# Spacing the indirect scatters of two routed layers with a small GpSimd clear

## The chip, the cores and the metric

The kernel runs on one core of one Trainium2 chip. The metric is the device time of one execution in microseconds (us). The engines are named as in the profile: PE is TensorE, PEld its weight loads, ACT is ScalarE, DVE is VectorE, POOL is GpSimd, SP is SyncE, which here only issues DMAs.

## What is computed

A two-layer transformer stack over 4096 tokens (16 sequences of 256) of width 128, all in float32. Each layer is an attention-like part and a feed-forward part that routes every token to a few experts, and each part is normalised and added to the residual:

```
x = x + layernorm(L0_attn(layernorm(x)))        # sorted-kernel attention, 16 heads
x = x + layernorm(L0_ffn(layernorm(x)))         # routed: 32 experts, top 4, gated SiLU, hidden 128, plus a shared one
x = x + layernorm(L1_attn(layernorm(x)))        # RWKV time mix and channel mix
x = x + layernorm(L1_ffn(layernorm(x)))         # routed: 8 experts, top 2, SiLU, hidden 512, plus a shared one
return x
```

The routed part of layer 0, cut:

```
logits = flat @ router_w.T + router_bias
topk_scores, topk_idx = top_k(softmax(logits), 4);  topk_scores /= topk_scores.sum()
h = silu(flat @ gate_w[e].T) * (flat @ up_w[e].T)
out = sum over the 4 chosen e of score * (h @ down_w[e].T)
out = out + silu(flat @ sgate_w.T) * (flat @ sup_w.T) @ sdown_w.T
```

## The kernel before

`build` runs the stages one after another, and `routed` builds both routed layers, with `layer` 0 (called gated) or 1. Only `routed` is touched.

The tokens stand in SBUF as 32 tiles of 128 tokens (`TILES`), in 8 groups of 4 (`GROUPS`, `TPG`), and are routed in two parts of 16 tiles each (`PT`). For each part DVE picks the experts (`choose`), counts them (`bases`) and works out the row of a sorted buffer to which each token goes (`place`). The end of `place` raises the semaphore `placed` (L1391). POOL waits for it (L965) and then scatters: for each tile and each chosen expert it issues one indirect DMA (L968) that writes the 128 rows of 512 bytes of a tile of `h_tok` to their places in the DRAM buffer `xs[part]`. That makes 16 tiles times 4 choices, 64 transfers, for a part of layer 0, and 32 for a part of layer 1. A run of such transfers is called a burst below.

In the meantime PE, ACT and DVE work on the shared expert: `shared_first` (L1031, three matmuls for each product, L1027 to L1029), ACT's SiLU (`shared`, L1220 in layer 0, L1224 in layer 1), in layer 0 DVE's product (L1416), and `shared_second` (L1052). There are 32 such units in a layer (`SU`). The three engines hand the work to each other by semaphores that each matmul group, activation and product raises: `gate_ps` and `up_ps` by PE for ACT and DVE, `sum_ps` by PE for DVE and ACT, `hidden_ready` for PE. The routing steps of part 1 are mixed in: the transposes and router products of the second half of the tokens (`turn` L994, `route` L1006, ACT's `turned` L1208 and L1209), then `bases(1)`, `place(1)` and `table(1)` at fixed unit numbers (`AT_TOTALS`, `AT_RANKS`, `AT_OWNERS`). In layer 1 eight units (`EARLY`) come ahead of this second half.

After the last shared unit comes the routed stage. SP loads 512 rows at a time of `xs` (L924), first when all scatters of that part have landed (L921), four buffers ahead (`XB`). PE turns them (L1095) and ACT copies them out (L1252, `e_x_turned`): this is the start of one quad of the routed stage. There are 24 quads for a part in layer 0 and 10 in layer 1 (`JQ`). The results are stored to `ys` (L930). When those of part 0 are stored, POOL gathers them with indirect DMAs (L979) and adds tiles to the residual (`residual_add`, L215). The order on POOL is thus: scatters of part 0, scatters of part 1, gathers. The gathers of part 1 of layer 0 are made in the next stage, `rwkv` (L1910).

Of the kernel before, what the change touches and what calls it, by code (L numbers as in the profile page):

```python
# [15 lines left out]
P = 128  # L16
# [24 lines left out]
FROM = 1  # L41
# [49 lines left out]
def build(nc, a, out):  # L91
    top = ExitStack()
    with top:
# [157 lines left out]
        attention0(nc, a, locals())  # L251
        clear_semaphores(100)
        routed(nc, a, locals(), 0)
        clear_semaphores(90)
        rwkv(nc, a, locals())
        clear_semaphores(100)
        routed(nc, a, locals(), 1)


# [523 lines left out]
def routed(nc, a, env, layer):  # L783
# [4 lines left out]
    E, K, SH, WE = ((E0, K0, SH0, WE0), (E1, K1, CH1, WE1))[layer]  # L788
# [19 lines left out]
    with ExitStack() as s:  # L808
        def tb(name, cols, dt=F32, rows=P):
            return s.enter_context(nc.sbuf_tensor(pre + name, [rows, cols], dt))  # L810
# [4 lines left out]
        sem = lambda n: env["semaphore"](pre + n)  # L815
# [5 lines left out]
        w_down = tb("w_down", SH * P)  # L821
        w_all = tb("w_all", E * WE)
        router, bias = tb("router", E), tb("bias", E) if gated else None
        zeros = tb("zeros", P)
        scale_y, shift_y, shift_x = tb("scale_y", TILES), tb("shift_y", TILES), tb("shift_x", TILES)
        logits, left = tb("logits", PT * LW), tb("left", PT * LW)
        best, chosen, total = tb("best", PT * 8), tb("chosen", PT * 8), tb("total", PT)
# [58 lines left out]
        x_ps, x_sb, first_ps, t_silu, t_hidden, h_ps, h_sb, y_ps, y_sb = map(  # L886
            sem, ("x_ps", "x_sb", "first_ps", "t_silu", "t_hidden", "h_ps", "h_sb", "y_ps", "y_sb"))
        weighed, combined, own = sem("weighed"), sem("combined"), sem("own")
        normed, x_ready = sem("normed"), sem("x_ready")
        x_stats_done = sem("x_stats_done") if gated else sem("out_stored")  # L890

        def tile(x, t):
            return x[:, t * P:(t + 1) * P]
# [4 lines left out]
        with nc.Block() as block:  # L898
# [44 lines left out]
            @block.gpsimd  # L943
            def _(pool):
                nc.gpsimd.memset(zeros[:, :], 0.0).then_inc(zeros_made, 1)
                nc.gpsimd.memset(ones_bf[:, :], 1.0).then_inc(constants, 1)
                nc.gpsimd.memset(later[:, :], -1.0).then_inc(constants, 1)
                nc.gpsimd.memset(one_row[:, :], 1.0).then_inc(constants, 1)
                flow3 = flow[:, :].rearrange("p (e t) -> p e t", t=PT)
                nc.gpsimd.memset(flow3[:, :, 0:1], 0.0).then_inc(constants, 1)  # L950
                nc.gpsimd.memset(flow3[:, :, 1:PT], 1.0).then_inc(constants, 1)
                nc.gpsimd.iota(tile_start[:, 0:1], pattern=[[P * P, 1]], base=0, channel_multiplier=P,
                               allow_small_or_imprecise_dtypes=True).then_inc(constants, 1)
                pool.wait_ge(constants, FROM + 6)
                nc.gpsimd.affine_select(out=later[:, :], in_=later[:, :], compare_op=ALU.is_ge, fill=0.0, base=0,
                                        pattern=[[-1, P]], channel_multiplier=1).then_inc(constants, 1)
                for i, (n, c) in enumerate(SPLIT):
                    pool.wait_ge(staged, FROM + 16 * len(SPLIT))
                    nc.gpsimd.tensor_copy(w_hi[n][:, :], w_stage[i][:, :]).then_inc(hi_made, 1)
                    pool.wait_ge(hi_made, FROM + i + 1)  # L960
                    nc.gpsimd.tensor_tensor(w_lo[n][:, :], w_stage[i][:, :], w_hi[n][:, :].bitcast(F32),
                                            ALU.subtract).then_inc(lo_made, 1)
                pool.wait_ge(cleared, FROM + 16 * NP)
                for part in range(NP):
                    pool.wait_ge(placed, FROM + part + 1)  # L965
                    for t in range(part * PT, (part + 1) * PT):
                        for k in range(K):
                            nc.gpsimd.indirect_dma_start(  # L968
                                out=xs[part], out_offset=bass.IndirectOffsetOnAxis(ap=rows_of[:, t * K + k:t * K + k + 1], axis=0),
                                in_=tile(h_tok, t), in_offset=None, bounds_check=ROWS - 1).then_inc(scattered[t // TPG], 16)  # L970
                for part in range(OVER):
                    last = (part + 1) * JQ
                    for i in range(YB):
                        pool.wait_ge(stored[i], FROM + 16 * ((last - 1 - i) // YB + 1))
                    for t in range(part * PT, (part + 1) * PT):
                        if t >= GB:
                            pool.wait_ge(combined, FROM + t - GB + 1)
                        for k in range(K):
                            nc.gpsimd.indirect_dma_start(  # L979
                                out=got[t % GB][:, k * P:(k + 1) * P], out_offset=None, in_=ys[part],  # L980
                                in_offset=bass.IndirectOffsetOnAxis(ap=rows_of[:, t * K + k:t * K + k + 1], axis=0),
                                bounds_check=ROWS - 1).then_inc(gathered[t % GB], 16)
                        g = t // TPG
                        if t % TPG == TPG - 1 and g % GPP:
                            env["residual_add"](pool, g - 1, normed, x_ready)
                    env["residual_add"](pool, (part + 1) * GPP - 1, normed, x_ready)
# [1039 lines left out]
```

## Time and profile before

| | |
|---|---|
| time, median of 3 runs | 1696.18 us (1694.03 to 1700.94) |
| time of the profiled execution | 1706.38 us |
| its span, first to last instruction | 1704.6 us |
| mean granted clock of PE | 0.756 |
| busy: PE, DVE, ACT, POOL | 987.1, 844.1, 612.4, 496.3 us (58, 50, 36, 29%) |
| scatters of layer 0 (L968), 128 | 126.6 us busy on POOL |
| scatters of layer 1 (L968), 64 | 63.6 us busy on POOL |

No engine is busy for much more than half of the span. The page shows shares of the whole; the question for this change is what PE, ACT and DVE do while POOL scatters, and what they wait for then. An indirect DMA's row on POOL is the time in which POOL writes its descriptors, not the time of the transfer.

### The profile page before, as it was taken

How to read it: one execution, taken by the hardware profiler on the slowest of the kernel's cores; microseconds unless marked ns; L12 is line 12 of the kernel's file. 1: busy time of each engine (PE TensorE's matmuls, PEld its weight loads, DVE VectorE, ACT ScalarE, POOL GpSimd, SP SyncE). 2: the span in 40 equal slices, each digit the busy share in tenths (PEclk: the TensorE clock that was granted, in tenths of full speed). 3: DMA queues.
4: the chain of work that ended last, by engine and by line, in shares of the span. 5: the costliest groups of instructions: out<-in, count | busy, mean ns of one | idle time of the engine just before them, and what ended most of it. 6: DMA issues, size and time to landing. Idle time of an engine off the chain costs nothing. (4 is left out here: it accounts for less than half of the span.)

```text
span 1704.6 us, 20367 instructions
## 1 busy us (share of the span) xinstructions
PE 987.1 (58%) x5710; PEld 749.2 (44%) x5712; DVE 844.1 (50%) x2487; ACT 612.4 (36%) x1263; POOL 496.3 (29%) x598
## 2 busy tenths in 40 slices
PE   2865666642215822898667224666525484998840
PEld 1624555532214721777556113343315472776630
DVE  4497688874503500632356338998844220002525
ACT  2331566645202200333222226566434332553420
POOL 0001333321571275001562564000001534004435
PEclk9995665665557955999899657787766596998975
DMA  2000000009511011344343210000052201122221
GB/s 59 0 1 0 0 0 0 0 1 288 207 52 39 13 51 35 93 121 132 100 123 84 71 42 25 1 1 1 1 146 98 65 21 53 51 64 61 56 65 53
DMA packets 130722, 96.98 MB, mean 57 GB/s; under 512 B 11600, under 2 KB 121552, under 8 KB 129616
## 3 DMA queue, kind: packets, MB, share of 16 engines
q1 hardware_dynamic: 118352, 70.79, 14.3%
q0 software_dynamic: 12288, 25.19, 5.0%
q8 instruction: 41, 0.67, 0.2%
q14 instruction: 41, 0.34, 0.1%
HBM read 45.61 MB, written 50.33 MB: 56 GB/s over the span
## 5 line engine op out<-in xcount | busy, mean ns | idle before, releaser
L968 POOL DMA_INDIRECT e_xs<-h_tok,rows_of x128 | 126.6, 989 | 147.3 <-DVEq L1391 108.9
L1520 DVE COPY e_y_rows<-e_ps_y 128x512 f32<-128x512 f32 x68 | 47.0, 691 | 242.4 <-PE e_ps_y L1152 167.5
L1052 PE MATMUL e_ps_y<-e_w_down,e_hidden 128*128 128x128 f32 x512 | 77.3, 300 | 120.5 <-DVE e_hidden L1416 110.5
L1052 PEld LDWEIGHTS e_ps_y<-e_w_down,e_hidden 128*128 128x128 f32 x512 | 74.3, 213 | 130.8 <-DVE e_hidden L1416 65.8
L979 POOL DMA_INDIRECT e_got<-e_ys,rows_of x64 | 65.0, 1015 | 175.1 <-DMA e_ys<-e_y_rows 132.1
L979 POOL DMA_INDIRECT e_got<-e_ys,e_rows_of x64 | 66.0, 1031 | 151.1 <-DMA e_ys<-e_y_rows 132.7
L632 ACT ACTIVATE mask<-ps_q,k_neg 128x256 bf16<-128x256 f32 x256 | 100.4, 485 | 21.0 <-PE ps_q L725 21.0
L1104 PE MATMUL e_ps_gu<-e_w_all,e_x_turned 128*128 x384 | 103.3, 416 | 2.6 <-ACT e_x_turned L1252 1.7
L1416 DVE TENSOR_TENSOR e_hidden<-e_ps_gu,e_silu 128x512 f32<-128x512 f32 x32 | 22.0, 690 | 155.8 <-remote 118.8
L968 POOL DMA_INDIRECT e_xs<-h_tok,e_rows_of x64 | 63.6, 994 | 105.3 <-DVEq L1391 86.4
L725 PE MATMUL ps_q<-q_parts,pick 128*128 (+1 forms) x256 | 66.1, 400 | 44.7 <-DVE mask L553 41.5
L1152 PE MATMUL e_ps_y<-e_w_all,e_h_turned 128*128 x640 | 87.2, 281 | 7.8 <-issue 5.2
L1134 PE MATMUL e_ps_up<-e_w_all,e_x_turned 128*128 x160 | 85.7, 620 | 9.5 <-ACT e_x_turned L1252 9.5
L553 DVE TENSOR_TENSOR mask<-ps_q,k_tok 128x1024 bf16<-128x1024 f32 x64 | 75.3, 1218 | 27.6 <-PE ps_q L725 25.4
L1123 PE MATMUL e_ps_y<-e_w_all,e_h_turned 128*128 x384 | 60.1, 304 | 46.5 <-ACT e_h_turned L1268 28.2
L1258 ACT ACTIVATE e_silu<-e_ps_gu 128x512 f32<-128x512 f32 x48 | 28.7, 597 | 161.6 <-PE e_ps_gu L1104 119.1
L1910 POOL DMA_INDIRECT c_got<-e_ys,rows_of x64 | 66.6, 1040 | 61.5 <-POOLq L106 21.6
L1220 ACT ACTIVATE e_silu<-e_ps_gu 128x512 f32<-128x512 f32 x32 | 19.1, 597 | 181.8 <-remote 131.8
L1268 ACT ACTIVATE e_h_turned<-e_ps_h 128x512 f32<-128x512 f32 x128 | 75.9, 593 | 22.2 <-remote 11.3
L1152 PEld LDWEIGHTS e_ps_y<-e_w_all,e_h_turned 128*128 128x128 f32 x640 | 79.9, 196 | 8.9 <-issue 8.8
L1263 ACT ACTIVATE e_hidden<-e_ps_up 128x512 f32<-128x512 f32 x80 | 47.7, 597 | 99.3 <-PE e_ps_up L1134 85.3
L1104 PEld LDWEIGHTS e_ps_gu<-e_w_all,e_x_turned 128*128 128x128 f32 x384 | 74.6, 205 | 17.0 <-issue 5.0
(367 smaller groups left out, 2455.2 us busy)
## 6 DMA issues: line engine op xcount, KB each, us to landing
e_x_rows<-e_xs SPq DMA_DIRECT2D x68, 256.0 KB, 3.1
e_ys<-e_y_rows SPq DMA_DIRECT2D x68, 256.0 KB, 2.4
e_xs<-e_zeros SPq DMA_DIRECT2D x2, 6144.0 KB, 34.7
e_w_all<-in_w SPq DMA_DIRECT2D x4, 1536.0 KB
e_xs<-e_zeros SPq DMA_DIRECT2D x2, 2560.0 KB
e_w_all<-in_w SPq DMA_DIRECT2D x4, 1024.0 KB, 11.1
e_xs<-h_tok,rows_of POOLq DMA_INDIRECT x128
result<-x_tok SPq DMA_DIRECT2D x8, 256.0 KB
```

Of the source, the lines that this page charges most:

```text
L553: last = nc.vector.tensor_tensor(mask[parity][quad][j][:, :].rearrange("p (h t) -> p h t", t=T), psq[0][:, :].rearrange("p (h t) -> p h t" ...
L632: last = nc.scalar.activation(mask[u][QS // 2 + j][keys][:, h * T:(h + 1) * T], psq[1][:, h * T:(h + 1) * T], ACT.Sign, bias=k_neg[u][:, k ...
L725: last = nc.tensor.matmul(psq[0 if on_dve else 1][:, h * T:(h + 1) * T], pick[:, (quad * HQ + h) * P:(quad * HQ + h + 1) * P], q_parts[:, ...
L968: nc.gpsimd.indirect_dma_start(out=xs[part], out_offset=bass.IndirectOffsetOnAxis(ap=rows_of[:, t * K + k:t * K + k + 1], axis=0), in_=til ...
L979: nc.gpsimd.indirect_dma_start(out=got[t % GB][:, k * P:(k + 1) * P], out_offset=None, in_=ys[part], in_offset=bass.IndirectOffsetOnAxis(a ...
L1052: last = nc.tensor.matmul(ps_sum[g % len(ps_sum)][:, t * P:(t + 1) * P], hidden[n % 2][:, t * P:(t + 1) * P], w_down[:, i * P:(i + 1) * P] ...
L1104: last = nc.tensor.matmul(ps_gu[n % 2][:, t * 2 * P:(t + 1) * 2 * P], x_turned[n % 2][:, t * P:(t + 1) * P], at(w_all, col, 2 * P), start= ...
L1123: last = nc.tensor.matmul(ps_y[:, o], h_turned[n % 2][:, o], at(w_all, col + 2 * P, P), start=True, stop=True)
L1134: nc.tensor.matmul(ps_up[n % 2][:, :], x_turned[q % 2][:, t * P:(t + 1) * P], at(w_all, col, CH1 * P), start=True, stop=True).then_inc(fir ...
L1152: last = nc.tensor.matmul(ps_yy[q % 2][:, t * P:(t + 1) * P], h_turned[n % 2][:, i * P:(i + 1) * P], at(w_all, col + (CH1 + i) * P, P), st ...
L1268: nc.scalar.activation(h_turned[n % 2][:, :], (ps_h if gated else ps_hh[n % 2])[:, :], ACT.Copy).then_inc(h_sb, 1)
L1910: nc.gpsimd.indirect_dma_start(out=got[t % GB][:, k * P:(k + 1) * P], out_offset=None, in_=env["ys0"], in_offset=bass.IndirectOffsetOnAxis ...
```

## The change

One tile of 256 columns (`spacer`) and one semaphore (`spaced`) are added. In the scatter loop, after each indirect DMA is issued, POOL clears this tile with a memset and waits for the end of that memset before it goes on. The loop runs 128 times in layer 0 and 64 times in layer 1, so 192 memsets and 192 waits are added. The gathers are as they were.

```diff
-        zeros = tb("zeros", P)
+        zeros, spacer = tb("zeros", P), tb("spacer", 256)
...
-        normed, x_ready = sem("normed"), sem("x_ready")
+        normed, x_ready, spaced = sem("normed"), sem("x_ready"), sem("spaced")
...
                             nc.gpsimd.indirect_dma_start(
                                 out=xs[part], out_offset=bass.IndirectOffsetOnAxis(ap=rows_of[:, t * K + k:t * K + k + 1], axis=0),
                                 in_=tile(h_tok, t), in_offset=None, bounds_check=ROWS - 1).then_inc(scattered[t // TPG], 16)
+                            nc.gpsimd.memset(spacer[:, :], 0.0).then_inc(spaced, 1)
+                            pool.wait_ge(spaced, FROM + t * K + k + 1)
```

## Rows read from the trace of the kernel before

**Rows 1.** Groups of POOL's instructions by line and shape, whole span.
```profile
line engine op names shapes xcount | busy us, mean ns | idle before us <-releasers
L968 POOL DMA_INDIRECT e_xs<-h_tok,rows_of x128 | 126.6, 989 | 147.3 <-DVEq L1391 108.9 <-issue 38.4
L968 POOL DMA_INDIRECT e_xs<-h_tok,e_rows_of x64 | 63.6, 994 | 105.3 <-DVEq L1391 86.4 <-issue 18.9
...
L653 POOL MEMSET qn<- 64x256 f32 x1 | 0.3, 306 | 109.4 <-POOLq L315 109.4
```

**Rows 2.** Timeline of POOL: start, duration, instruction, idle time before it and releaser.
```profile
521.26 0.98 POOL L968 DMA_INDIRECT e_xs<-h_tok,rows_of  x1 [0.30 <-issue]
585.34 0.98 POOL L968 DMA_INDIRECT e_xs<-h_tok,rows_of  x1 [63.10 <-DVEq L1391]
...
666.38 0.98 POOL L968 DMA_INDIRECT e_xs<-h_tok,rows_of  x1 [0.31 <-issue]
...
1312.18 1.09 POOL L968 DMA_INDIRECT e_xs<-h_tok,e_rows_of  x1 [51.14 <-DVEq L1391]
...
1352.73 1.11 POOL L968 DMA_INDIRECT e_xs<-h_tok,e_rows_of  x1 [0.30 <-issue]
1389.12 0.98 POOL L968 DMA_INDIRECT e_xs<-h_tok,e_rows_of  x1 [35.28 <-DVEq L1391]
```

**Rows 3.** Busy time of each engine in stretches with and without scatters.
```profile
core 0: us, PE busy (x) PEld busy (x) DVE busy (x) ACT busy (x) POOL busy (x), PEclk, DMA share, GB/s
440.00:450.00 10.00, 0.00 (x0) 0.00 (x0) 9.31 (x40) 0.47 (x2) 7.56 (x9) 0.50 0.68 280
...
533.00:560.00 27.00, 26.93 (x155) 23.48 (x155) 16.98 (x76) 9.77 (x14) 0.00 (x0) 0.94 0.00 1
...
645.00:655.00 10.00, 0.00 (x0) 0.00 (x0) 0.00 (x0) 0.00 (x0) 7.56 (x9) 0.50 0.13 46
```

**Rows 4.** Timelines of PE, ACT and DVE about the scatters of layer 0.
```profile
479.51 0.63 PE L1029 MATMUL e_ps_gu<-e_h_hi,e_sgate_hi 128*128 128x512 f32 x1
...
475.64 0.60 ACT L1208 ACTIVATE e_h_hi<-e_ps_x 128x512 fp32r<-128x512 f32 x1 [12.99 <-remote]
...
527.47 0.60 ACT L1220 ACTIVATE e_silu<-e_ps_gu 128x512 f32<-128x512 f32 x1 [49.44 <-remote]
...
671.90 0.69 DVE L1416 TENSOR_TENSOR e_hidden<-e_ps_gu,e_silu 128x512 f32<-128x512 f32 x1 [36.41 <-remote]
...
685.85 0.60 ACT L1252 ACTIVATE e_x_turned<-e_ps_x 128x512 f32<-128x512 f32 x1 [3.67 <-PE e_ps_x L1095]
```

**Rows 5.** Timeline of ACT about the scatters of layer 1.
```profile
1351.17 0.60 ACT L1208 ACTIVATE e_h_hi<-e_ps_x 128x512 fp32r<-128x512 f32 x1 [15.63 <-DMA e_xs<-h_tok,rows_of]
...
1357.67 0.60 ACT L1224 ACTIVATE e_hidden<-e_ps_up 128x512 f32<-128x512 f32 x1 [4.11 <-remote]
...
1430.30 0.60 ACT L1252 ACTIVATE e_x_turned<-e_ps_x 128x512 f32<-128x512 f32 x1 [28.40 <-remote]
```

**Rows 6.** Timeline of ACT later in the routed stage of layer 0.
```profile
798.31 0.60 ACT L1252 ACTIVATE e_x_turned<-e_ps_x 128x512 f32<-128x512 f32 x1
```

**Rows 7.** Timelines of POOL and ACT at the ends of two gather bursts.
```profile
819.20 1.01 POOL L979 DMA_INDIRECT e_got<-e_ys,rows_of  x1 [0.30 <-issue]
...
822.46 0.60 ACT L1258 ACTIVATE e_silu<-e_ps_gu 128x512 f32<-128x512 f32 x1 [8.68 <-remote]
...
1585.02 1.02 POOL L979 DMA_INDIRECT e_got<-e_ys,e_rows_of  x1 [0.30 <-issue]
1586.06 1.28 POOL L215 TENSOR_TENSOR x_tok<-x_tok,y_tok 128x512 f32<-128x512 f32 x1
1587.50 1.03 POOL L979 DMA_INDIRECT e_got<-e_ys,e_rows_of  x1 [0.16 <-issue]
...
1587.26 0.60 ACT L1263 ACTIVATE e_hidden<-e_ps_up 128x512 f32<-128x512 f32 x1 [0.99 <-remote]
```

**Rows 8.** Timeline of POOL: an instruction that waits for the one before it.
```profile
4.63 0.28 POOL L248 TENSOR_SCALAR_AFFINE_SELECT ident<-ident 128x128 f32<-128x128 f32 x1 [0.24 <-POOL ident L246]
```

## The prediction

> **What bounds the kernel now.** I began with the groups of POOL's instructions [rows 1]: a scatter takes POOL 0.99 us, 128 times in layer 0 and 64 times in layer 1. The timeline of POOL [rows 2] adds the 0.30 us between any two of them, so that one starts every 1.29 us, and the four bursts: in layer 0 64 transfers that end at 522.2 and 64 from 585.3 to 667.4, in layer 1 32 from 1312.2 to 1353.8 and 32 from 1389.1 on, 41 us long, to 1430. POOL waits for nothing within them. By this alone, POOL would be on the path that sets the end only where its landing is late.
>
> The busy times by stretch [rows 3] say more. Between two bursts (533 to 560) PE is busy for all of its 27 us and its granted clock is 0.94 of full speed. Within a burst (645 to 655) PE, ACT and DVE do nothing at all for ten microseconds, and the clock stands at 0.50, the lower level of 1.2 GHz. They aren't out of work: the shared expert's units are left. The timelines [rows 4] show what they wait for. PE starts the last matmul of the first gate product at 479.51 and ends it at 480.1. ACT needs just this for its SiLU, has been free since 478, and starts at 527.47, after 49.4 us for which the profile finds no releaser ("remote"). This is 5 us after the end of the burst. The same holds for ACT at 475.64 (13.0 us), for DVE at 671.90 (36.4 us; 4.5 us after the end of the second burst) and in layer 1 [rows 5] for ACT at 1351.17, 1357.67 and 1430.30 (15.6, 4.1 and 28.4 us). Each of these waits is for a semaphore that PE raises. So what bounds both routed layers while POOL scatters is neither POOL's work nor PE's, but hand-offs from PE that reach the others late. Yet early in a burst all goes well: DVE is busy for 9.31 of the 10 us from 440 on [rows 3].
>
> **Does the rate of the transfers matter?** The hand-offs are free again some time after the burst's last transfer, and the longer the burst, the later. I take the last indirect DMA's end on POOL to the first held step. Gathers [rows 7]: 8 in a row, 1586.0 to 1587.26, 1.2 us; 16 in a row, 820.2 to 822.46, 2.3 us. Scatters: 32 in a row, 1353.84 [rows 2] to 1357.67 [rows 5], 3.8 us; 64 in a row, 667.4 [rows 2] to 671.90 [rows 4], 4.5 us, and 5.2 us after the other burst of 64. Less the 1.2 us of the shortest burst, 1.0, 2.6 and 3.3 us are left for 16, 32 and 64. It looks like a backlog that grows with each transfer, by 0.05 to 0.1 us (3.3 / 64 and 2.6 / 32). Whatever holds PE's hand-offs would then need about 1.34 to 1.40 us for a transfer that comes every 1.29 us. This is an estimate from four ends of bursts; what the queue is, the trace doesn't show.
>
> **The change part by part.** *The memset.* No 128x256 memset stands in the trace; one of 64x256 takes 0.306 us [rows 1], and I take 0.31. *The wait on it.* POOL begins another kind of instruction 0.02 us after an indirect DMA (L215 at 1586.06) and an indirect DMA 0.16 us after that one [rows 7]; where it waits for its own last result it starts 0.24 us after it [rows 8]. The gap of 0.30 us ahead of the next DMA stays or is partly used up. So the period grows from 1.29 us by at least 0.31 + 0.02 + 0.16 - 0.30 = 0.19 us and at most by 0.31 + 0.30 + 0.24 = 0.85 us. I take 0.40 us, a period of 1.69 us, the memset with a short wait behind a gap that stays. *What is queued behind the wait:* only POOL's next scatter, and after the last one the gathers, which wait for stores over 100 us later. *The bursts' lengths:* 64 x 0.40 = 26 us more for each of layer 0 and 32 x 0.40 = 13 us for each of layer 1, together 77 us. *DVE and the memset:* POOL's instructions and DVE's run side by side from 440 to 450 without loss [rows 3], but those have no memset among them. At worst each memset holds DVE for 0.31 us while DVE is on the path, which at the starts of the bursts is some 10 times, 3 us. I take nothing.
>
> With a period of 1.69 us and a need of 1.40 us the backlog never forms, and what I forecast is that the hand-offs then pass. Where does the path go?
>
> *Layer 0.* ACT's step at 475.64 comes 12 us earlier (13.0 us less the 1 us that the transposes take), the first SiLU by 47.3 us more (480.1 to 527.47), together 59: the units begin at 468. From 527.5 to 585.3 they ran unheld up to the end of `place(1)`; the same 58 us lead to 526. But POOL is late next: its first burst now ends at 522.2 + 26 = 548. The second runs from 548 to 548 + 64 x 1.69 = 656. The units run on beside it. By the code 11 are left behind `place(1)`; 155 matmuls in 27 us [rows 3], 14 to a unit, give 2.4 us each, so 27 us and 4 us for the first load and turn: the routed stage begins at 557, not at 685.85 [rows 4]. Its quads come every (798.31 - 685.85) / 26 = 4.3 us [rows 4, 6], so the 24 of part 0 last until 661, and the second burst, landed at 657, isn't waited for by much. I take 128 us less.
>
> *Layer 1.* The 15.6 us and the 4.1 us [rows 5] shrink by 14 and 2, the 28.4 us and some 2 us of lateness just ahead of it go: 46 us less. The bursts end at 1367 and, from 1373 on, at 1427; the routed stage begins at 1384 with 10 quads of part 0, longer than that.
>
> The sum is 128 + 46 = 174 us. Since a hand-off can still meet a transfer, and the routed stage of part 0 now runs beside the second burst, I give 10 us back. 1706.4 - 174 + 10 = 1542 us for a profiled execution. The median of the runs stands 10.2 us below the profiled one, of which I take 7: 1535 us.
>
> **The rivals.** *No relief, slower.* The held hand-offs may need silence and not a lower rate. At 1587.26 ACT was freed 1.2 us after the gather's end and 0.24 us before the next one began [rows 7]. Spacing leaves only 0.30 + 0.40 = 0.70 us of silence between two transfers. If 1.2 us are needed, each burst holds PE's hand-offs as before, but 26, 26, 13 and 13 us longer: 1696.2 + 77 = 1773 us, a little less if some units slip through in the longer bursts. It decides at the point where the gap falls short of what the queue needs. For it speaks that hand-offs are also late within short gather bursts, which leave no backlog; against it the growth with the burst's length. The Trainium skill, "SBUF — State Buffer", section "SBUF: two separate sides", says that engine ports and DMA ports are disjoint and that neither side can be slowed by the other. By that rule the scatters wouldn't be the cause of PE's waits, nothing would be freed, and the spacers would only cost, which ends at the same 1773 us; the idle stretch in [rows 3] speaks against it here.
>
> *Partial relief.* Without the backlog the hand-offs may be late as they are in the gather bursts, with single waits like the 8.7 us of [rows 7]. Then a unit of three hand-offs takes perhaps 5 to 7 us within a burst. Some 10 to 15 units would pass in the 80 us from 468 to 548 where now almost none does, and the second burst, 26 us longer, takes part of it back: 20 to 45 us less in layer 0, about nothing in layer 1. That is 1650 to 1676 us; I set it at 1655.
>
> *The change does not do what it says.* If POOL overlapped the memset with the descriptors, the period would stay below 1.34 us and the time at 1696. The wait on `spaced` all but excludes this.
>
> **How the numbers follow.** Relief 0.50 (1515 to 1600), partial relief 0.18 (1600 to 1688), no relief 0.27 (1720 to 1785), no change 0.05. 1535 us is the time of the likeliest. For 8 in 10 the range must reach past partial relief into the milder part of no relief, in which units slip through: 1515 to 1755 us. The likeliest case by itself spans 1515 to 1600. A measurement of this kernel can tell about 0.5% from no change. Faster by more than that 0.67, within it 0.06, slower 0.27.
>
> **What would show it.** Right: scatters start every 1.6 to 1.8 us; between 480 and 548 PE is busy and its clock goes to the upper level; no "remote" wait of ACT or DVE over 5 us in the bursts; the routed stage of layer 0 starts near 557. Wrong: the first SiLU of layer 0 starts only after the first burst's end, near 553, which is no relief; or a wait of POOL on its own memset of over 0.5 us, since POOL's semaphore would then be held like PE's. Also wrong would be a routed stage that runs slowly beside the second burst, which cuts the 128 us.

## The result, and the profile after

The changed kernel takes 1572.55 us (1570.67 to 1579.18), the kernel before beside it 1695.11 us: a ratio of 0.928 with a 95% interval of 0.9255 to 0.9305. It is 123 us faster, where 161 us were forecast. The profiled execution takes 1570.78 us, its span is 1569.0 us, 135.6 us less than before.

The groups of POOL's instructions after the change, against [rows 1]:

```profile
L968 POOL DMA_INDIRECT e_xs<-h_tok,rows_of x128 | 129.1, 1008 | 146.0 <-POOL e_spacer L971 96.8 <-DVEq L1393 45.8 <-issue 3.5
...
L968 POOL DMA_INDIRECT e_xs<-h_tok,e_rows_of x64 | 63.6, 994 | 101.7 <-DVEq L1393 52.2 <-POOL e_spacer L971 48.4 <-issue 1.1
L971 POOL MEMSET e_spacer<- 128x256 f32 x192 | 62.5, 325 | 0.2
```

The clears themselves are 62.5 us, 0.325 us each. POOL's idle time behind them is more: 96.8 and 48.4 us, 145.2 us in all. The timeline of POOL after the change, against [rows 2], shows it one by one, with the last scatter of layer 0 and the first of layer 1:

```profile
444.80 0.99 POOL L968 DMA_INDIRECT e_xs<-h_tok,rows_of  x1 [0.78 <-POOL e_spacer L971]
445.79 0.33 POOL L971 MEMSET e_spacer<- 128x256 f32 x1
446.89 1.02 POOL L968 DMA_INDIRECT e_xs<-h_tok,rows_of  x1 [0.78 <-POOL e_spacer L971]
...
709.93 0.99 POOL L968 DMA_INDIRECT e_xs<-h_tok,rows_of  x1 [0.78 <-POOL e_spacer L971]
...
1226.83 1.09 POOL L968 DMA_INDIRECT e_xs<-h_tok,e_rows_of  x1 [52.22 <-DVEq L1393]
```

The clear starts the moment the indirect DMA ends, and the next DMA starts 0.78 us after the clear. One transfer comes every 2.10 us, not every 1.69. The two bursts of layer 0 have run together into one of 128 that lasts to 711 us.

The timeline of ACT after the change, against [rows 4]: the first SiLU, and the first step of the routed stage for part 0 and for part 1. Between them stand SP's first loads of `xs`.

```profile
469.71 0.60 ACT L1222 ACTIVATE e_silu<-e_ps_gu 128x512 f32<-128x512 f32 x1 [2.31 <-PE e_ps_gu L1031]
...
576.41 4.62 SPq L924 DMA_DIRECT2D e_x_rows<-e_xs  x5
...
580.81 0.60 ACT L1254 ACTIVATE e_x_turned<-e_ps_x 128x512 f32<-128x512 f32 x1 [31.99 <-PE e_ps_x L1097]
...
716.51 0.60 ACT L1254 ACTIVATE e_x_turned<-e_ps_x 128x512 f32<-128x512 f32 x1 [31.64 <-PE e_ps_x L1097]
```

The hand-offs pass: the first SiLU starts at 469.7 instead of 527.5. But there are two new waits of 32 us each, behind PE's turns of rows, which wait for the loads of `xs`, which wait for the last scatter of their part (POOL: 709.93 + 0.99; ACT: 716.51). The busy times by stretch, against [rows 3], show both: the columns are PE, PEld, DVE, ACT, POOL, then the granted clock, the DMA share and GB/s. The first row is of the kernel before, the others are of the changed one.

```profile
440.00:550.00 110.00, 34.83 (x161) 30.36 (x162) 26.87 (x103) 20.42 (x37) 63.02 (x64) 0.58 0.19 69
...
440.00:550.00 110.00, 89.71 (x496) 77.23 (x495) 59.93 (x193) 34.18 (x60) 69.64 (x104) 0.84 0.15 56
550.00:575.00 25.00, 0.88 (x8) 0.68 (x7) 0.69 (x1) 0.00 (x0) 15.61 (x24) 0.59 0.09 32
...
680.00:711.00 31.00, 3.78 (x23) 2.99 (x21) 2.08 (x3) 2.15 (x5) 19.46 (x30) 0.63 0.09 30
```

PE is busy for 90 of the 110 us from 440 on, where before it was for 35, most of that behind the first burst. Then it is idle twice while POOL still scatters. Layer 1's first scatter tells how the gain divides: it starts at 1226.83 instead of 1312.18 [rows 2], so layer 0 and what follows it gave 85.4 us; from there to the end of the span it takes 342.2 instead of 392.4 us, so layer 1 gave 50.2 us.

Not all hand-offs pass. ACT and DVE still have 27 remote waits, 98.7 us in all and 11.2 us at the longest. None lies within the scatters; all lie in the bursts of gathers or just behind them, which the change leaves as they were.

### The profile page after: what moved, and what is told of

The parts are those of the page before. It is cut to its first block and busy times, and to the rows that moved or that the text cites. A ratio compares the mean times of both kernels' runs of the same rounds, so it can differ in the third digit from the quotient of the medians.

```text
span 1569.0 us, 20563 instructions
## 1 busy us (share of the span) xinstructions
PE 971.8 (62%) x5712; PEld 741.5 (47%) x5712; DVE 845.7 (54%) x2487; ACT 612.6 (39%) x1263; POOL 564.6 (36%) x790
## 5 line engine op out<-in xcount | busy, mean ns | idle before, releaser
L968 POOL DMA_INDIRECT e_xs<-h_tok,rows_of x128 | 129.1, 1008 | 146.0 <-POOL e_spacer L971 96.8
L1260 ACT ACTIVATE e_silu<-e_ps_gu 128x512 f32<-128x512 f32 x48 | 28.7, 599 | 161.4 <-PE e_ps_gu L1106 127.6
L1513 DVE TENSOR_TENSOR e_hidden<-e_ps_gu,e_silu 128x512 f32<-128x512 f32 x48 | 33.1, 690 | 89.1 <-ACT e_silu L1260 75.1
L1097 PE MATMUL e_ps_x<-ident,e_x_rows 128*128 128x128 f32 x272 | 43.2, 283 | 60.7 <-DMA e_x_rows<-e_xs 31.2
L996 PE MATMUL e_ps_x<-ident,h_tok 128*128 128x128 f32 x64 | 17.8, 434 | 100.8 <-ACT h_tok L1204 100.8
```

Source lines behind the costliest of these rows:

```text
L968: nc.gpsimd.indirect_dma_start(out=xs[part], out_offset=bass.IndirectOffsetOnAxis(ap=rows_of[:, t * K + k:t * K + k + 1], axis=0), in_=til ...
L1097: last = nc.tensor.transpose(ps_x[q % len(ps_x)][:, o], x_rows[q % XB][:, o], ident[:, :])
```

## Experiments

Theory A is that of the prediction: hand-offs of PE are held while indirect DMAs come at a higher mean rate than something can take. Its rivals are B (the clear's work matters, not the time) and C (a silence after each transfer matters, not the mean rate). D and E ask what in a transfer counts, its bytes or its descriptors. F came up on the way: the holding is not the kernel's own. The experiments carry short names, e1 to e13.

**A clear of one column (e1).** Against the changed kernel:

```diff
-    nc.gpsimd.memset(spacer[:, :], 0.0).then_inc(spaced, 1)
+    nc.gpsimd.memset(spacer[:, 0:1], 0.0).then_inc(spaced, 1)
```

> The clear shrinks from 128x256 to 128x1; the wait behind it stays. Theory A (rate: PE's hand-offs pass as soon as a transfer comes less often than every 1.34 to 1.40 us, whatever fills the pause): the period falls from 2.10 us to 0.99 + 0.06 + 0.78 = about 1.83 us, no hand-off is held, and the two bursts of layer 0 end near 558 and 676 us instead of 575 and 711. Part 1 of the routed stage of layer 0 then starts about 36 us earlier; layer 1, whose bursts are off the path, is unchanged. That is 1572 - 36 = about 1537 us. Theory B (it is the clear itself, its 0.32 us of POOL's work, that keeps the queue open, not the time between transfers): hand-offs are held again for 10 us and more, and the time is 1600 us or above.

**The wait behind the next transfer (e2).**

```diff
-    nc.gpsimd.memset(spacer[:, :], 0.0).then_inc(spaced, 1)
-    pool.wait_ge(spaced, FROM + t * K + k + 1)
+    if t * K + k:
+        pool.wait_ge(spaced, FROM + t * K + k)
+    nc.gpsimd.memset(spacer[:, :], 0.0).then_inc(spaced, 1)
```

> The clear keeps its 128x256, but the wait for it moves behind the next transfer (POOL waits for the clear before, not for the one just issued). The gap between two transfers is then the clear and the 0.30 us, without the 0.78 us of the wait. Theory A (rate; need 1.34 to 1.40 us): the period is 1.29 + 0.33 = 1.62 us, the hand-offs pass freely, the bursts of layer 0 end near 545 and 649 us, the routed stage starts near 556, and part 1 near 660 instead of 716: 1572 - 56 = about 1515 us. Theory C (silence: what holds the hand-offs needs a pause of about 1 us after each transfer, as the 1.11 us in the changed kernel): 0.63 us is not enough, hand-offs are held by 10 us and more within the bursts, and the time is 1700 us or above.

**A clear after every fourth transfer (e4).**

```diff
-    nc.gpsimd.memset(spacer[:, :], 0.0).then_inc(spaced, 1)
-    pool.wait_ge(spaced, FROM + t * K + k + 1)
+    if (t * K + k) % 4 == 3:
+        nc.gpsimd.memset(spacer[:, :], 0.0).then_inc(spaced, 1)
+        pool.wait_ge(spaced, FROM + (t * K + k) // 4 + 1)
```

> The clear and its wait come after every fourth transfer only, so that three gaps of 0.30 us are followed by one of 1.11 us. Theory A (rate): the mean period is 1.29 + 0.81 / 4 = 1.49 us, above the 1.34 to 1.40 us that are needed; a hand-off waits at most for the backlog of four transfers, 4 x 0.1 = 0.4 us. The bursts of layer 0 end near 536 and 631 us, so that part 0 starts at 556 and part 1 at 660, behind the quads: about 1515 us. Theory C (silence after each transfer): a hand-off waits for the one long gap in each 6.0 us, some 3 us on the mean; a unit of three hand-offs takes 9 us instead of 2.3 and only some 8 of 32 units pass in the first burst. The time is 1620 us or above.

**Rows of 64 bytes, no clear (e5).** Against the kernel before:

```diff
-    out=xs[part], out_offset=...
-    in_=tile(h_tok, t), ...
+    out=xs[part].rearrange("r (a c) -> (r a) c", c=16), out_offset=...
+    in_=tile(h_tok, t)[:, 0:16], ...
```

> The kernel before, without any clear, but each of the 128 rows of a scatter is 64 bytes long instead of 512: only the first 16 of 128 values of a token are written, and the rows stand closer together in the buffer, so that the sorted buffer holds other data. The number of descriptors and POOL's work stay. Theory D (bytes: the data of the transfers hold the hand-offs): the waits marked remote of 49 us and 36 us in layer 0 vanish, the period stays 1.29 us, the bursts end near 522 and 604, and the time falls to about 1500 us. Theory E (descriptors: their number or POOL's writing of them holds the hand-offs): the same remote waits of 10 to 50 us stay and the time is within 1% of 1696 us.

*Measured, all on chip 9.* The chips are numbered as the results give them; the place of the first profiles has no number. The kernel before took 1440.84 us there (1437.43 to 1444.09), not 1696 us. e1 took 1477.01 us (ratio 1.0246, 1.0218 to 1.0275), e2 1440.66 us (1.0003, 0.9991 to 1.0016), e4 1442.52 us (1.001, 0.9997 to 1.0022), e5 1443.19 us in one execution. None of the four profiles has a remote wait of ACT or DVE over 0.4 us. So they decide nothing between A to E, whose expected times all started from held hand-offs. They do give POOL's prices. First e1, then e2, in the timeline of POOL:

```profile
446.91 0.12 POOL L971 MEMSET e_spacer<- 128x1 f32 x1
447.81 0.98 POOL L968 DMA_INDIRECT e_xs<-h_tok,rows_of  x1 [0.78 <-POOL e_spacer L971]
```

```profile
445.73 0.33 POOL L973 MEMSET e_spacer<- 128x256 f32 x1
446.23 0.99 POOL L968 DMA_INDIRECT e_xs<-h_tok,rows_of  x1 [0.17 <-issue]
```

The 0.78 us belong to the wait, whatever the size of the clear; behind a late wait the DMA follows after 0.17 us. The period of e2 is 1.48 us: its 0.33 us clear partly stands in the 0.30 us gap that was there before, and adds 0.19 us.

**The two kernels once more (e6, e7).** The question is now whether the 255 us between 1696 and 1441 belong to the kernel.

> The kernel before itself, once more with its profile. Beside the last four kernels it took 1440.8 us, not 1696 us, and none of these four shows a remote wait of over 0.4 us. Theory F (condition: the held hand-offs belong to the chip or the hour in which the first profiles were taken, and not to the kernel): where the time is near 1441 us, the profile has the same 128 + 64 scatters every 1.29 us, and no remote wait of ACT or DVE over 1 us; where it is near 1696 us, the remote waits of 49 us and 36 us are back. Theory A as first held (a backlog that any burst at 1.29 us builds up) would have the remote waits in every profile of this kernel, whatever its time.

> The changed kernel itself, once more. Theory F: where the kernel before takes 1441 us, nothing is there to be freed, and the spacers only cost. The bursts of layer 0 end at 711 us instead of 609 us, and part 1 of the routed stage starts at 716 us, 27 us later than with the 128x1 clear (690 us, 1477 us): 1477 + 27 = about 1504 us, 4.4% slower than before. Where the kernel before takes 1696 us, it is 1572 us again, 7% faster. Theory A as first held: 1572 us and faster in either case.

*Measured, on chip 7.* The kernel before 1438.33 us (its profiled execution 1442.33 us), the changed kernel 1501.85 us: ratio 1.0444 (1.0427 to 1.0462), **slower**. Theory F holds. The busy times from 470 to 523 us, of the kernel before as first profiled and then of the same kernel on chip 7:

```profile
470.00:523.00 53.00, 6.28 (x20) 5.06 (x20) 0.69 (x1) 2.37 (x3) 40.04 (x41) 0.53 0.15 52
```

```profile
470.00:523.00 53.00, 51.60 (x302) 44.02 (x300) 35.24 (x128) 16.35 (x25) 40.55 (x41) 0.98 0.15 52
```

POOL issues 41 scatters in both, and the DMA share (0.15) and 52 GB/s are the same; PE does 20 matmuls in one and 302 in the other, with a granted clock of 0.53 (the lower level but for a little) and 0.98 (the upper). The first scatters of layer 1, in e6 and in e7, show where the changed kernel loses:

```profile
1114.41 1.09 POOL L968 DMA_INDIRECT e_xs<-h_tok,e_rows_of  x1 [51.37 <-DVEq L1391]
```

```profile
1175.18 1.09 POOL L968 DMA_INDIRECT e_xs<-h_tok,e_rows_of  x1 [51.19 <-DVEq L1393]
```

60.8 us are lost up to there, and from there to the end of the span nothing (325.0 against 326.2 us). Layer 0's routed stage starts at 580 and part 1 at 715 us in e7, within 1.1 us of where they start in the first profile after: POOL sets them in either condition.

I call a chip *holding* if its remote waits are there (the kernel before near 1700 us) and *free* otherwise. Chips 7 and 9 were free, chips 2, 3 and 4 below were holding, as was the place of the first profiles.

**Four kinds of spacing in one kernel (e8).**

```diff
+    MIX = {(0, 0): ('late', 256, 1), (0, 1): ('own', 256, 4), (1, 0): ('late', 64, 1), (1, 1): ('own', 256, 8)}
...
+    kind, cols, every = MIX[layer, part]
+    if kind and (t * K + k) % every == every - 1:
+        if waited < made:
+            pool.wait_ge(spaced, FROM + made)
+        nc.gpsimd.memset(spacer[:, 0:cols], 0.0).then_inc(spaced, 1)
+        made += 1
+        if kind == "own":
+            pool.wait_ge(spaced, FROM + made)
+            waited = made
```

and behind each gather of layer 1 a clear of 256 columns with the late wait.

> Four kinds of spacing in one kernel: part 0 of layer 0 a clear of 128x256 whose wait comes behind the next transfer (a transfer every 1.48 us), part 1 a clear with its own wait after every fourth transfer (1.49 us on the mean); part 0 of layer 1 a clear of 128x64 with the late wait (1.3 to 1.48 us, not yet measured), part 1 one clear with its wait after every eighth transfer (1.39 us on the mean). The gathers of layer 1 get the clear with the late wait too, those of layer 0 stay as they were. Where the kernel before takes 1441 us (no hand-off is held in it): none is held here either, and the time is 1441 + 0.19 x 32 = about 1447 us, since only the last 32 gathers lie on the path. Where it takes 1696 us (hand-offs held): theory A (rate) frees part 0 and part 1 of layer 0 and part 0 of layer 1, and at 1.39 us part 1 of layer 1 is the edge; the time is about 1500 us. Theory C (silence of 1 us behind each transfer) leaves the waits marked remote of 36 to 50 us in layer 0 and 15 to 28 us in layer 1, and the time is 1690 us or above.

*Measured, on chip 2, holding:* 1538.62 us, the kernel before 1690.72 us, one execution each. The waits of ACT and DVE within the scatters or just behind them, in the order part 0 of layer 0 (one), part 0 of layer 1 (its burst ends at 1208) and the two longest of part 1 of layer 1:

```profile
496.91 0.60 ACT L1236 ACTIVATE e_silu<-e_ps_gu 128x512 f32<-128x512 f32 x1 [2.32 <-remote]
```

```profile
1202.58 0.60 ACT L1224 ACTIVATE e_h_hi<-e_ps_x 128x512 fp32r<-128x512 f32 x1 [12.85 <-DMA e_xs<-h_tok,rows_of]
...
1210.63 0.69 DVE L1437 COPY y_tok<-e_ps_y 128x512 f32<-128x512 f32 x1 [5.64 <-remote]
```

```profile
1277.49 0.60 ACT L1279 ACTIVATE e_hidden<-e_ps_up 128x512 f32<-128x512 f32 x1 [6.45 <-remote]
...
1286.03 0.60 ACT L1279 ACTIVATE e_hidden<-e_ps_up 128x512 f32<-128x512 f32 x1 [6.49 <-remote]
```

At 1.48 us, one hand-off in a burst of 64 is late. Part 1 of layer 0, where three gaps of 0.30 us out of four stay and the mean is 1.49 us, has none at all. Theory C falls: what counts is the mean over some transfers, not the silence after each. The two spacings of layer 1, 1.31 us and a clear after every eighth transfer, still hold. The wait of 12.85 us is the one that the kernel before has at 1351.17 [rows 5], 15.6 us; the profile puts both down to a DMA, but the code waits there only for PE's `fm_ps`. Theory B falls as well: a clear of 0.17 us behind every transfer holds, and one of 0.33 us behind every fourth, half as much clearing, frees. The unspaced gathers of layer 0 hold ACT's SiLU six times, for 4.9 to 10.0 us, and DVE for up to 12.1 us; those of layer 1, spaced, hold nothing.

The periods named so far are those of the regular pattern. Some gaps are longer, at the starts of bursts above all. Counted from the first transfer of a burst to its last, the means of the four bursts are 1.50, 1.51, 1.35 and 1.37 us.

**Gathers too (e9)** is e2 with this behind each gather but the last 32 of layer 1, and likewise in the next stage:

```diff
+    if gated or part == 0:
+        pool.wait_ge(spaced, FROM + NP * PT * K + t * K + k)
+        nc.gpsimd.memset(spacer[:, :], 0.0).then_inc(spaced, 1)
```

> Every scatter gets the 128x256 clear with the late wait (a transfer every 1.48 us), and so does every gather but the last 32 of layer 1, behind which nothing of PE is left. Where hand-offs are held (the kernel before near 1691 us), theory A (mean rate; 1.48 us is slow enough, as both parts of layer 0 showed with four kinds of spacing) expects no remote wait of ACT or DVE over 1 us from the gathers either. The kernel with four kinds of spacing lost 52 us up to the start of layer 1 (1129 against 1077 us) to the unspaced gathers and 46 us in layer 1 to spacings of 1.31 and 1.39 us; without them 1538 - 98 = about 1441 us, and with gathers that take 0.18 x 64 = 11 us longer per burst 1441 to 1455 us, 15% faster than before. Where the hand-offs are free (before near 1440 us), only the longer gathers are left: 1441 to 1452 us. If gathers hold PE for another reason than their rate, the remote waits of 5 to 10 us in the gathers stay, and the time is 1490 us or above where before takes 1691 us.

**Bytes and rates (e10)** is e8 with another table, without clears in the gathers, and with e5's rows of 64 bytes in part 0 of layer 0:

```diff
-    MIX = {(0, 0): ('late', 256, 1), (0, 1): ('own', 256, 4), (1, 0): ('late', 64, 1), (1, 1): ('own', 256, 8)}
+    MIX = {(0, 0): (None, 0, 1), (0, 1): ('late', 128, 1), (1, 0): ('late', 192, 1), (1, 1): ('late', 128, 1)}
```

> Four bursts once more. Part 0 of layer 0 has no clear (a transfer every 1.29 us), but its rows are 64 bytes long instead of 512, so that its part of the sorted buffer holds other data. Part 1 of layer 0 and part 1 of layer 1 have a clear of 128x128 with the late wait (1.31 us with 64 columns and 1.48 with 256, so some 1.38 us), part 0 of layer 1 one of 128x192 (some 1.43 us). Where hand-offs are held: theory D (the bytes of a transfer hold them) expects ACT's first SiLU of layer 0 at 470 us, theory E (its descriptors do) at about 527 us as in the kernel before. By theory A with a need of 1.34 to 1.40 us, 1.43 us is free of remote waits over 3 us and 1.38 us has at most single ones of 2 to 6 us, where 1.31 us had one of 5.6 us behind a burst of 32. Where hand-offs are free, nothing of this shows and the time is about 1442 us.

*Measured, on chip 3, holding:* before 1704.58 us, e9 1514.8 us (0.8877, 0.8837 to 0.8917), e10 1674.26 us in one execution. ACT and POOL in e10:

```profile
528.21 0.60 ACT L1234 ACTIVATE e_silu<-e_ps_gu 128x512 f32<-128x512 f32 x1 [48.78 <-remote]
...
652.38 0.60 ACT L1234 ACTIVATE e_silu<-e_ps_gu 128x512 f32<-128x512 f32 x1 [24.76 <-remote]
```

```profile
592.28 0.99 POOL L971 DMA_INDIRECT e_xs<-h_tok,rows_of  x1 [0.17 <-issue]
593.27 0.22 POOL L980 MEMSET e_spacer<- 128x128 f32 x1
593.65 0.99 POOL L971 DMA_INDIRECT e_xs<-h_tok,rows_of  x1 [0.17 <-issue]
```

With an eighth of the bytes ACT's first SiLU is held for 48.8 us, as with all of them (49.4, [rows 4]). Theory D falls, E stands: the number of transfers or descriptors matters, not the data; which of the two, no run separates. At 1.37 us between transfers (1.41 us on the mean of that burst) hand-offs are still held, for up to 24.8 us; my edge of 1.34 to 1.40 us was too low. At 1.43 us (1.46 on the mean) the one remote wait near that burst of 32 is 0.97 us.

e9 missed its 1441 to 1455 us by 60 us, and its time lies where gathers were to hold PE for another reason than their rate (1490 us or above). The waits of ACT and DVE in it, as line, what it waited for, us in all, times, longest:

```profile
DVE e_y_rows L1526 <- remote: 24.5, 7, 4.5
ACT e_silu L1264 <- remote: 12.9, 3, 4.6
ACT e_silu L1226 <- remote: 11.2, 5, 3.1
```

No remote wait is over 4.6 us, where that other reason was to leave 5 to 10 us in the gathers. But on this chip 1.48 us lets single waits through all along the second burst of scatters too, where the quads need nearly 7 us instead of 4.3.

**A longer clear (e11, e12) and the changed kernel beside them (e13).** e11 is e2 and e12 is e9, both with a tile of 512 columns:

```diff
-        zeros, spacer = tb("zeros", P), tb("spacer", 256)
+        zeros, spacer = tb("zeros", P), tb("spacer", 512)
```

> Scatters only, as in the changed kernel, but a clear of 128x512 with the late wait: 0.12 us and 0.0008 us for each column make some 0.55 us, so a transfer every 1.70 us. That is the period which the prediction assumed (1.69 us). Where hand-offs are held (before near 1700 us): if only the period was mis-sized there, the routed stage of layer 0 starts near 557 us and its part 1 near 661 us, no remote wait over 3 us lies within the scatters, and the time is about 1535 us or, with the unspaced gathers costing what they did with four kinds of spacing, 1441 + 52 + 20 = about 1513 us; it beats the changed kernel by 40 to 60 us. If 1.70 us is still too short (1.48 us let single waits of up to 4.6 us through in the last runs), the quads beside the second burst take over 5 us each and it is 1560 us or above. Where hand-offs are free: the bursts end at 549 and 658 us, behind other work, and the time is 1441 us, as with the 256 columns.

> The same clear of 128x512 with the late wait behind all scatters and behind all gathers but the last 32 of layer 1. Where hand-offs are held: at 1.70 us none is, in scatters or gathers; what the 1.48 us left (54 us up to the start of layer 1) goes, while a burst of 64 gathers takes 26 us longer. Between 1450 and 1490 us, 13 to 15% faster than before and faster than the 1515 us of the clears of 256 columns. If the longer bursts of gathers are on the path, 1500 us or above. Where hand-offs are free, only that lengthening is left: 1441 to 1480 us.

> The changed kernel once more, beside the two others and the kernel before on the same chip. Where hand-offs are held (before near 1700 us): about 1572 us, 7% faster, with the routed stage of layer 0 at 581 us and its part 1 at 716 us. Where they are free (before near 1440 us): about 1502 us, 4% slower, with the same two starts, since these are set by POOL's 2.10 us per transfer in either case.

*Measured, on chip 4, holding:* before 1697.71 us; e11 1521.75 us (0.8959, 0.8922 to 0.8997); e12 1482.73 us (0.8727, 0.8698 to 0.8755); the changed kernel 1570.65 us (0.9251, 0.9212 to 0.9291). POOL's period in e11, the first step of its routed stage and the first scatter of its layer 1:

```profile
503.72 0.99 POOL L968 DMA_INDIRECT e_xs<-h_tok,rows_of  x1 [0.17 <-issue]
504.71 0.54 POOL L973 MEMSET e_spacer<- 128x512 f32 x1
505.41 0.99 POOL L968 DMA_INDIRECT e_xs<-h_tok,rows_of  x1 [0.17 <-issue]
```

```profile
553.99 0.60 ACT L1255 ACTIVATE e_x_turned<-e_ps_x 128x512 f32<-128x512 f32 x1 [5.70 <-PE e_ps_x L1098]
```

```profile
1175.77 1.09 POOL L968 DMA_INDIRECT e_xs<-h_tok,e_rows_of  x1 [51.12 <-DVEq L1394]
```

The first scatter of layer 1 in e13, beside it:

```profile
1222.06 1.09 POOL L968 DMA_INDIRECT e_xs<-h_tok,e_rows_of  x1 [51.12 <-DVEq L1393]
```

e11 has a transfer every 1.70 us, and no remote wait of ACT or DVE lies within its scatters. The routed stage starts at 554 us, and its second part follows without the 32 us pause. What is left lies in the gathers, which e11 leaves unspaced; here by line, what it waited for, us in all, times, longest:

```profile
ACT e_silu L1261 <- remote: 28.1, 4, 9.3
DVE e_y_rows L1523 <- remote: 22.8, 4, 8.6
```

e12 spaces these as well, and has no remote wait of any engine; 39 us more are gained. In the stretch from 560 to 635 us, beside the second burst, e9 (1.48 us, chip 3), then e12 (1.70 us, chip 4) and last e2 (1.48 us as in e9, but on the free chip 9):

```profile
560.00:635.00 75.00, 47.35 (x255) 39.41 (x253) 30.34 (x45) 19.03 (x33) 65.59 (x100) 0.91 0.37 112
```

```profile
560.00:635.00 75.00, 67.70 (x412) 57.57 (x413) 39.90 (x59) 27.10 (x52) 67.71 (x89) 1.00 0.54 155
```

```profile
560.00:635.00 75.00, 68.18 (x418) 58.06 (x419) 37.69 (x57) 27.04 (x52) 64.10 (x97) 1.00 0.57 163
```

PE does 255 matmuls in e9, 412 in e12 and 418 in e2. So 1.70 us on chip 4 loses next to nothing, and 1.48 us does on chip 3. How much of that difference belongs to the chip and how much to the period isn't shown, since no two of these spacings ran on one holding chip for this stretch. e12 beats the kernel before and the changed one on a holding chip; it was not run on a free one, where its longer bursts of gathers should cost something. e2, which costs nothing on a free chip, was not run whole on a holding one.

## Why the prediction was right, and where it was not

**The bound.** Right for where the profile was taken: each of the remote waits that the prediction named is gone in the profile after. Wrong in what it took for granted, that they are a property of this kernel. The same kernel with the same 192 scatters runs 255 us faster on chips 7 and 9, and there the change costs 4.4%. The sign of the forecast was right where hand-offs are held and would have been wrong on chips 7 and 9. That both kernels of the result met the condition of the first profile was luck: the prediction gave the other one no chance, and nothing in a profile from one place tells how another will do.

One of its readings says less than it claims. DVE's 9.31 of 10 us from 440 on [rows 3] were to show that hand-offs pass early in a burst, but PE has no instruction in that stretch, so there was nothing to hand over.

**Rate, not silence.** The estimate from the ends of bursts had the right kind: e8 (mean of four, free) and e10 (1.37 us, evenly spaced, held) decide it. The size was low: 1.34 to 1.40 us was read; with a transfer every 1.37 us, 1.41 us on the mean, waits of up to 24.8 us stay, 1.43 us nearly frees a burst of 32, 1.48 us leaves one late hand-off on chip 2 and many of 2 to 4.6 us on chip 3, and 1.70 us leaves none on chip 4. The chips differ here, so the edge is known for each only from its own run. Since the changed kernel went far past this, the error cost nothing.

**The period, the term that was mis-sized.** The clear was right (0.31 forecast, 0.325 measured). The wait was put at 0.16 us behind another instruction [rows 7] or 0.24 us behind POOL's own result [rows 8], and the whole at +0.40 us within 0.19 to 0.85. Measured is +0.81: a DMA behind a wait for the clear starts 0.78 us after it. The row of [rows 8] was of another kind of instruction, a plain POOL operation and no indirect DMA. The prediction had named a wait of over 0.5 us as a sign that POOL's semaphore is held as well; that reading is wrong, since e1 on a free chip has the same 0.78 us. The bursts grew by 192 x 0.81 = 156 us, not by 77. The other term that was put at nothing, what a clear costs DVE, was small: DVE is busy for 845.7 us after and for 844.1 before.

**Layer 0.** The units came as forecast: first SiLU 469.7 (forecast 468). Then POOL was late by the wrong term. The first burst's rows could be loaded from 576.4 on (SP's first load of `xs`) instead of 548, so the routed stage started at 580.8, not 557; the second landed at 712 instead of 657, so part 1 started at 716.5, 32 us after PE had run out of quads, where the prediction had it "not waited for by much". 85.4 us were gained, not 128. That the period makes the difference, e11 shows, which has the period that the forecast assumed: its routed stage starts at 554 where 557 was forecast, and 1312.2 - 1175.8 = 136.4 us are gained. Of these some 5 us belong to the place, since the changed kernel is that much earlier there as well (1222.1 against 1226.8). The quads themselves ran beside the burst at their full pace, one every 4.3 us.

**Layer 1.** 50.2 us against 46. The shared units outlast its first burst and the quads of part 0 its second, so the wrong period did no harm; e11 gained 392.4 - 346.3 = 46.1 us.

**The sum.** 85.4 + 50.2 = 135.6 us, the difference of the spans. e11 gives 136.4 + 46.1 = 182.5, against a forecast of 174 less the 10 given back; its median of 1521.75 us is 13 us below the 1535 us, about the 10 us that were given back for hand-offs that still meet a transfer. In e11 none does within the scatters.

**The rivals.** "No relief" fell with the first SiLU at 469.7, and with it, where hand-offs are held, the strict reading of what the Trainium skill says in "SBUF — State Buffer", section "SBUF: two separate sides". What e10 shows agrees with the page as far as it goes: an eighth of the bytes changed nothing, so the amount of data that moves isn't what counts. What is held is the hand-off, of which that section doesn't speak. The Trainium skill's "Perfetto Trace Analysis", section "Tensor Engine Instruction (MATMUL, LD_WEIGHTS)", puts a step in which the semaphore update spreads to all engines behind the end that the profile reports; the waits of up to 49.4 us lie behind that reported end, though no run here shows in which step. "Partial relief" with its single waits is what the unspaced gathers still show (up to 11.2 us in the changed kernel), and e9 at 1.48 us.

**What stays open.** Which part of a holding chip delays PE's hand-offs, and whether holding belongs to the chip or to the hour. Five numbered chips were each seen in one condition only, and none was seen twice at different hours. In order of time the runs were holding (the first place), free (9, 7) and holding (2, 3, 4), so either reading fits.

## What to carry to other kernels

A spacer pays only up to the point at which the burst it lengthens outlasts the work beside it: here the bursts at 1.70 us per transfer ended about when that work did (554 and 660 us), those at 2.10 us outlasted it by 32 us each time, and the surplus of 0.40 us cost 46 us up to the start of layer 1's scatters (1222.1 in e13 against 1175.8 in e11, on one chip). Put the wait for a dummy instruction behind the next transfer rather than ahead of it, so that a clear of 256 columns costs 0.19 us per transfer, as in e2, and not 0.81. And where a profile shows idle engines with waits that it can't put down to anyone, run the kernel before on another chip first: the same change was worth 7% on one and cost 4% on the next.

## What the runs showed of the hardware

- A kernel of one core has two conditions that differ by chip or hour, 1438 to 1441 us and 1691 to 1705 us. Within a burst of scatters the number of transfers and the bytes moved are the same in both (41 transfers and 52 GB/s from 470 to 523 us). On one chip its executions lie within 1.5% of each other.
- An indirect DMA that follows a wait for POOL's own clear starts 0.78 us after it, for clears of 128x1 and of 128x256 alike, and on free and holding chips alike.
- A clear without that wait costs less than it lasts: 0.33 us add 0.19 us to the period, and the idle time ahead of the next indirect DMA falls from 0.30 to 0.17 us. A clear of 128x1 still takes 0.12 us, of 128x128 0.22 and of 128x512 0.54.
- On a holding chip the delay depends on the number of indirect transfers in a stretch (or of their descriptors) and not on their bytes: 48.8 us with rows of 64 bytes, 49.4 with 512. Waits of up to 24.8 us stay at a mean of 1.41 us per transfer (chip 3), at 1.50 us one of 2.3 us in a burst of 64 (chip 2) or many of up to 4.6 us (chip 3), and at 1.70 us none (chip 4).
